# A four-block transformer and GRU kernel: the last block's conditioning moved into the top-k stage, its first rows kept on chip, value projections in four banks, recurrent weights split by GpSimd

## The reference

```python
x = x + _L0_cond_ref(fside_BxSx1_0, cond_2048[:, None, :], x, 5120)     # mask of the 5120 largest of 512x512
x = _L1_cond_ref(x, ...)    # rmsnorm(x)*(1+scale)+shift, qkv, 16 heads of 32, softmax, o + o @ W_out, added to x
x = x + _L2_cond_ref(cond_2048, x, ...)   # a GRU over 512 steps, state 512, weights W_ih and W_hh 512x1536
x = _L3_cond_ref(x, cond_2048, ...)
# L3: ada = (timestep_embed @ ada_w + ada_b);  shift1, scale1, gate1, shift2, scale2, gate2 = split(ada, 6)
#     x1 = ln(x)*(1+scale1)+shift1;  qkv = x1 @ qkv_w + qkv_b;  16 heads of 128;  attn_out @ out_w + out_b
#     x = x + gate1*attn_out;  x2 = ln(x)*(1+scale2)+shift2
#     h = gelu(x2 @ ffn_w1 + ffn_b1);  x = x + gate2*(h @ ffn_w2 + ffn_b2)
```

## Time and profile before

| | |
|---|---|
| median of three runs | 4207.34 us |
| profiled execution | 4210.57 us (span 4208.9 us) |
| top-k stage | 0 to 311.9 us |
| small attention | 311.9 to 971.4 |
| splitting of GRU weights | 971.4 to 998.0 |
| gate inputs | 998.0 to 1152.7 |
| GRU, 512 steps and turning back | 1152.7 to 2594.9 |
| conditioning of the last block | 2594.9 to 2639.5 |
| last block | 2639.5 to 4208.9 |
| PE busy | 3731.0 us (89%) |
| DVE busy | 2778.2 us (66%) |
| ACT busy | 2086.6 us (50%) |
| POOL busy | 461.4 us (11%) |

### The profile page before, as it was taken

One profiled execution on the slowest core, in us unless ns is written; L12 is line 12 of the kernel. 1 busy time (PEld: TensorE's weight loads), 2 busy tenths in 40 slices (PEclk: granted clock), 3 DMA queues, 4 the chain that ended last, 5 costly groups with the idle time before them and its releaser, 6 DMA issues. The chain is left out here.

```text
span 4208.9 us, 177781 instructions
## 1 busy us (share of the span) xinstructions
PE 3731.0 (89%) x70140; PEld 2793.1 (66%) x70140; DVE 2778.2 (66%) x10585; ACT 2086.6 (50%) x7601; POOL 461.4 (11%) x397
## 2 busy tenths in 40 slices
PE   0537888876899999999999998799999999999999
PEld 0424564553499999999999996366456545654664
DVE  6886787785677777777777775376347626743762
ACT  2007786785755555555555552254235324532542
POOL 4005374370000000000000000000100100010001
PEclk9999999998955555555555556899999999999999
DMA  2002131231000000000000004310231122122102
GB/s 90 0 23 69 57 122 59 64 116 61 1 6 6 6 6 6 6 6 6 6 6 6 6 6 172 142 45 16 88 133 45 41 105 90 30 81 116 44 16 90
DMA packets 114611, 209.69 MB, mean 50 GB/s; under 512 B 44154, under 2 KB 76922, under 8 KB 112000
## 3 DMA queue, kind: packets, MB, share of 16 engines
q1 hardware_dynamic: 114436, 207.35, 14.5%
HBM read 165.35 MB, written 33.57 MB: 47 GB/s over the span
## 5 line engine op out<-in xcount | busy, mean ns | idle before, releaser
L1366 PE MATMUL gru_sum_n<-gru_state_parts,w_hh_hi 128*128 128x8 f16 x8192 | 500.2, 175 | 0.0
L1356 PE MATMUL gru_sum_n<-gru_state_parts,w_hh_lo 128*128 128x4 f16 x8192 | 489.4, 168 | 0.0
L1366 PEld LDWEIGHTS gru_sum_n<-gru_state_parts,w_hh_hi 128*128 128x128 f16 x8192 | 376.7, 104 | 0.0
L1356 PEld LDWEIGHTS gru_sum_n<-gru_state_parts,w_hh_lo 128*128 128x128 f16 x8192 | 376.7, 104 | 0.0
L528 ACT ACTIVATE dit_prob<-dit_bank,dit_head_nbias 128x512 f32<-128x512 f32 x256 | 176.0, 688 | 352.2 <-DVE dit_head_nbias L546 351.8
L1499 DVE TENSOR_TENSOR_SCAN gru_n_in<-gru_reset_gate,gru_sum_n 128x32 f32<-128x32 f32 x1024 | 225.5, 220 | 54.6
L1356 PE MATMUL gru_sum_rb<-gru_state_parts,w_hh_lo 128*128 128x4 f16 x4096 | 261.3, 169 | 0.0
L1366 PE MATMUL gru_sum_za<-gru_state_parts,w_hh_hi 128*128 128x8 f16 x4096 | 254.5, 169 | 0.0
L1366 PE MATMUL gru_sum_zb<-gru_state_parts,w_hh_hi 128*128 128x8 f16 x4096 | 254.5, 169 | 0.0
L1366 PE MATMUL gru_sum_ra<-gru_state_parts,w_hh_hi 128*128 128x8 f16 x4096 | 254.5, 169 | 0.0
L1356 PE MATMUL gru_sum_zb<-gru_state_parts,w_hh_lo 128*128 128x4 f16 x4096 | 252.4, 166 | 0.0
(11 more groups left out here) (320 smaller groups left out, 12547.4 us busy)
## 6 DMA issues: line engine op xcount, KB each, us to landing
dit_w_qk<-w_qk_parts SPq DMA_DIRECT2D x64, 512.0 KB, 3.7
weights<-w_parts SPq DMA_DIRECT2D x8, 4096.0 KB, 12.6
weights<-w_out_parts SPq DMA_DIRECT2D x5, 4096.0 KB, 15.6
weights<-w_v_parts SPq DMA_DIRECT2D x5, 4096.0 KB, 12.2
small_given_w<-in_L_cond_qkv_w SPq DMA_DIRECT2D x48, 256.0 KB, 3.1
w_qk_parts<-small_parts_w SPq DMA_DIRECT2D x32, 256.0 KB, 2.1
small_given_w<-in_L_cond_ffn_w SPq DMA_DIRECT2D x32, 256.0 KB, 3.7
w_parts<-small_parts_w SPq DMA_DIRECT2D x32, 256.0 KB, 2.4
```

The costliest lines, as they stand in the source:

```text
L1356: mm = pe.matmul(columns[:, j, 0], w_hh[1][:, k, c:c + P], parts[:, par, 0, k, :, LAST], start=opens, stop=False, skip_group_check=True)
L1366: mm = pe.matmul(columns[:, j], w_hh[0][:, k, c:c + P], parts[:, par, :, k, :, LAST], start=opens, stop=False, skip_group_check=True)
```

## The change

- The last block's conditioning moves into the top-k stage, behind the small attention's conditioning. SP loads ada_w in six pieces of 1 MB into the space of the search's keys, once the search is over; ACT takes the rows from PSUM and adds biases as it writes the columns; DVE adds the gates' bias at the end of the ranking and SP stores the gates. The stage `dit_condition_phase` is gone.
- One piece of SBUF, `room`, 128 KB per partition, is used in turn by the top-k's values and keys, small attention's intermediate tiles, the gate inputs of the GRU and the last block's weights. `given` (batch 0's rows) is allocated outside the stages.
- Small attention's value projections go to `bank[0]` to `bank[3]`, without waits between them; ACT first finishes all queries and keys and then copies the four value banks; DVE takes the low parts last.
- W_hh is split by GpSimd inside the gate-input stage, in eight pieces of 128x768, two behind each batch's copies of X. `split_weights` handles W_ih alone.
- At the end of the GRU SP loads out_w and the value weights into `room` as soon as the last gate inputs are taken. Batches are turned back in the order 1, 2, 3, 0, and batch 0 stays in `given`.
- In the last block PE maps the value bias (48 products, now 128 rows wide, in bank 7) in two halves around the turning of the first rows. DVE adds the result to the bias rows before values are projected. GpSimd's first work of a batch waits for `yl_ready`. out_w is loaded at the end of the batch before.

```diff
@@ topk_phase, sync
+            ada_w = a["L3_cond_ada_w"].rearrange("(k p) n -> p k n", p=P)
+            for i, j in enumerate(CHUNKS):
+                if i >= 4:
+                    sp.wait_ge(ada_rows, i - 3)
+                sp.dma_start(ada[i % 4], ada_w[:, :, j * D:(j + 1) * D]).then_inc(ada_loaded[i % 4], 16)
...
+            sp.wait_ge(gate_added, 1)
+            sp.dma_start(gates_dram, row[:, 4:6, :]).then_inc(gates_stored, 16)
+            sp.wait_ge(gates_stored, 16)
@@ topk_phase, scalar
+            for i in range(6):
+                act.wait_ge(ada_rows, i + 1)
+                act.activation(row[:, i, :], row_sum[i % 2][0:B, :], ACT.Copy).then_inc(row_ready, 1)
+            act.wait_ge(ada_cols, 1)
+            for i in range(4):
+                for f in range(KD):
+                    act.activation(dit_mod[:, i, f, :], col_sum[:, i, f, :], ACT.Identity, scale=XS,
+                                   bias=ada_shift[:, i, f:f + 1]).then_inc(dit_mod_made, 1)
@@ topk_phase, tensor
+            for i in range(6):
+                pe.wait_ge(ada_loaded[i % 4], 16 * (i // 4 + 1))
+                if i >= 2:
+                    pe.wait_ge(row_ready, i - 1)
+                for k in range(KD):
+                    mm = pe.matmul(row_sum[i % 2][0:B, :], c_T[:, k, :], ada[i % 4][:, k, :], start=(k == 0),
+                                   stop=(k == KD - 1))
+                mm.then_inc(ada_rows, 1)
...
@@ topk_phase, vector
+            for i in range(4):
+                dve.tensor_scalar(ada_shift[:, i], ada_b[:, CHUNKS[i] * KD:(CHUNKS[i] + 1) * KD],
+                                  1.0 if i in (SCALE1, SCALE2) else 0.0, XS, ALU.add, ALU.mult)
...
+            dve.wait_ge(row_ready, 6)
+            dve.wait_ge(gate_b_loaded, 32)
+            dve.tensor_tensor(row[:, 4:6, :], row[:, 4:6, :], gate_b, ALU.add).then_inc(gate_added, 1)
@@ small_attention_phase
+        out_of = [qkv_bank[n % 2] if n < first_v else bank[t] for n, (t, j) in enumerate(projections)]
...
-                    pe.wait_ge(bank_free, b * 12 + n + 1)
-                    if n >= first_v + 2:
-                        pe.wait_ge(vl_ready, b * TT + (n - first_v))
+                    if n < first_v:
+                        pe.wait_ge(bank_free, b * first_v + n + 1)
...
-                pe.wait_ge(vl_ready, (b + 1) * TT + 1)
                 pe.wait_ge(lo4_again, (b + 1) * TT * 2)
                 turn_qk(0)
+                pe.wait_ge(vl_ready, (b + 1) * TT)
...
-                    if n == first_v:
+                    if n == first_v - 1:
+                        low_again(TT - 2)
                         root(TT - 1)
-                        low_again(TT - 2)
-                    if n == first_v + 1:
                         high_parts(TT - 1)
-                low_again(TT - 1)
+                        low_again(TT - 1)
@@ gate_input_phase, gpsimd
+            def split_piece(j):
+                k, cols = pieces[j]
+                w = stage[:, j % SLOTS, :]
+                pool.wait_ge(piece_loaded[j % SLOTS], 16 * (j // SLOTS + 1))
+                pool.tensor_scalar(w, w, RS, None, ALU.mult).then_inc(piece_scaled, 1)
+                pool.wait_ge(piece_scaled, j + 1)
+                pool.tensor_copy(w_hh[0][:, k, cols], w).then_inc(piece_hi, 1)
+                pool.wait_ge(piece_hi, j + 1)
+                pool.tensor_tensor(w_hh[1][:, k, cols], w, w_hh[0][:, k, cols], ALU.subtract).then_inc(piece_lo, 1)
...
+                for j in range(b * per_batch, (b + 1) * per_batch):
+                    split_piece(j)
@@ gru_phase, sync
+            for v in range(2):
+                sp.wait_ge(now_loaded[v], 16 * (T // (2 * NOW)))
+            sp.dma_start(region[1], store.out.rearrange("p e k n -> p e (k n)")).then_inc(first_loaded, 16)
+            sp.dma_start(region[0], store.v.rearrange("p e k n -> p e (k n)")).then_inc(first_loaded, 16)
             xo = x_out.rearrange("b (t p) d -> p (b t) d", p=P)
-            for b in range(B):
-                sp.wait_ge(added, (b + 1) * TT)
+            for i, b in enumerate(later[:-1]):
+                sp.wait_ge(added, (i + 1) * TT)
                 sp.dma_start(xo[:, b * TT:(b + 1) * TT, :], X[:, b * TT:(b + 1) * TT, :]).then_inc(stored, 16)
-            sp.wait_ge(stored, 16 * B)
+            sp.wait_ge(stored, 16 * (B - 1))
@@ dit_phase
-            sp.dma_start(given[:], x_rows[:, 0, :, :]).then_inc(x_loaded, 16)
...
+            def map_bias(heads):
+                for h in heads:
+                    left = lambda v: v[:, h:h + 1].broadcast_to([P, P])
+                    mm = products(pe, bank[7][:], (left(bvh), left(bvl)), (w_out[:, 0, h, :], w_out[:, 1, h, :]),
+                                  h == 0, h == H - 1)
+                return mm
+
+            pe.wait_ge(bv_ready, 1)
+            pe.wait_ge(wo_loaded, 16)
+            map_bias(range(H // 2))
             turn_rows(0)
+            map_bias(range(H // 2, H)).then_inc(mapped, 1)
+            pe.wait_ge(rows_ready, 1)
...
+                pool.wait_ge(yl_ready, (b + 1) * KD)
                 pool.wait_ge(gates_loaded, (b + 1) * 16)
```

272 lines of the change are left out of this document (125 added, 147 removed).

## The result

Four runs of the changed kernel took 4129.34 to 4134.21 us, median 4132.31, beside 4209.41 of the kernel before (4205.28 to 4212.84); the ratio is 0.9814, 95% interval 0.9802 to 0.9826. Forecast were 4138, range 4123 to 4162. A second set of four runs gave 4130.57 to 4137.85, median 4132.71, ratio 0.9817 (0.9801 to 0.9834).

A forecast was written before the change was run, and what follows sets the result against it. TensorE is busy 89% of the span, but barriers separate stages, so edits were priced per stage: +2.8 - 16.2 - 10.9 + 4 - 49.2 = -69.5, from 4210.6 to 4141.1 us; 3.2 lower for the median, forecast 4138, range 4123 to 4162.

The forecast's parts named there:

- Top-k: Top-k stage: added conditioning hides beside VectorE's ranking; gates' bias add and store behind it cost +2.8 us.
- Small attention: Small attention: four value projections without waits start each batch's heads 4.05 us earlier, -16.2 us in four batches.
- The third rival: Small attention's units: TensorE stays at the lower clock, up to +108 us, 4246; chance 0.02.
- Splitting: Splitting of the GRU's weights: the stage ends after W_ih alone, -10.9 us, bounds -12 and -8.
- Gate inputs: GRU's gate inputs: GpSimd's splitting of W_hh slows VectorE beside it, +4 us, bounds 0 and +27.
- L1166 loses 0.8 - 0.5 = 0.3 in some four cycles a batch: Gate inputs: fixed 0.8 us per VectorE instruction beside GpSimd, half a microsecond spare; 16 x 0.3 = 5 us.
- the first rival: Gate inputs: GpSimd shuts VectorE out, the stage grows 14 to 27 us, not 4; about 4152, chance 0.12.
- GRU's end: GRU's end: region loads, then three stores ending about 2590.4; last block's first SP issue at 2595.5 us.
- The second rival: GRU's end: queues move 237 GB/s, not 425, so the last block starts 22 us later; 4160, chance 0.12.
- Start of the last block: Last block's start: the first value product begins 22.4 us after the stage's first SP issue.
- the bias decides: Last block's start: mapping the value bias, not the rows' shorter chain, sets the first value product, by 2 us.
- The rest of the last block: Last block's stage: its share of the -49.2 us forecast for GRU's end and the block's start, -5.2 us.

The follow-up runs named there:

- the kernel with two banks: The changed kernel with small attention's value projections in two banks again, copies and low parts in the order of before: 4150.98 us.
- twenty tiny ones: The changed kernel with twenty 4x4 products on TensorE behind the conditioning in top-k, results unread: 4122.36 us.
- the same again: The changed kernel run and profiled a second time with no edit: median 4132.71 us.
- four subtractions: The changed kernel with each of GpSimd's eight subtractions for W_hh done four times: 4135.27 us.
- values late: The changed kernel with the value weights (4.2 MB) loaded in the last block's stage behind its parameters, not at the GRU's end: 4131.22 us.
- one product: The changed kernel with one product instead of the 48 that map the value bias, its share of the output left out: 4132.56 us.
- the large products: The changed kernel with twenty more large float32 products on TensorE in top-k, behind the last block's conditioning, results unread: 4123.07 us.

## Why the prediction held, term by term

- *Top-k*, +2.8 (its terms as written add up to 2.7): +3.5 and +3.2. The order of events was as told; the store's way to the next stage was 0.8 us longer than the earlier trace rows gave for another store.
- *Small attention*, -16.2: the four banks bring 4.5 and not 4.05 in a batch, 18 in all, as the kernel with two banks shows; the stall, which no row of before has, takes 1.3 to 5 back. The third rival (the clock stays low in the units) did not come: the heads of a batch take 103.3 to 103.9 us in both kernels.
- *Splitting*, -10.9: -10.6 and -9.9.
- *Gate inputs*, +4: nothing that can be told, and 153.5 and 154.9 us where the prediction looked for 155 to 160. The step that failed is "L1166 loses 0.8 - 0.5 = 0.3 in some four cycles a batch" as a cost of the stage. L2115's growth stood for a price per instruction; measured it is 0.14 in the mean, and VectorE's idle time takes it. The same idle time is why the first rival fell.
- *GRU's end*: the stage starts 13.7 us behind the first store, where 14.8 were forecast. The second rival fell: beside the GRU's last steps the region loads moved at 401 GB/s, not 237, as the stretch from their issue to the first store says:

```profile
2538.00:2555.00 17.00, 15.74 (x441) 14.81 (x438) 11.96 (x72) 7.61 (x48) 0.00 (x0) 0.50 0.97 401
```

- *Start of the last block*: 22.3 against 22.4. The agreement to 0.1 is luck, since unedited starts spread from 21.95 to 23.94. That the bias decides, by about 2 us, holds: without it the values come 1.3 to 3.3 us sooner.
- *The rest of the last block*: its -5.2 came to -6.4 and -9.5. Beyond the forecast are the dips of the clock, four in before, three and one in the changed kernel, at 1.5 us each; the wait for w_qk, for which nothing was forecast, went from 4.3 and 3.9 to 4.7 and 4.8.
- *Not in the sum*: 4.5 us in the loop of the GRU. With it the sum would have been -74.

So the mechanisms held, and the error of 7.6 us has these parts: +4 charged for a contention that an idle engine absorbed, 4.5 from a loop whose instructions the change leaves as they were, and 1 to 4 in the last block, mostly the clock; against them the stall took back up to 5 that nobody had forecast. That the whole came within 6 us of 4138 owes something to that.

## What to carry to other kernels

A price per instruction, taken from where two engines meet, is a cost of the stage only if the slower one has no idle time there: read its idle column before adding it up. When an edit's gain does not match its mechanism, run the same number of instructions without the work; here twenty tiny ones gave the whole 10 us. And what is small and needed first is better issued ahead of what is large: the parameters behind 8.4 MB cost 10.5 us here, the head weights behind the next batch's rows 4.7 us of waiting at most.

## What was not expected of the hardware

- The same TensorE instructions stall for 2.6 to 3.0 us at one place in some executions and not in others, in this batch or that. Behind three of the six stalls seen (in the changed kernel, in the same again and with four subtractions) the clock stands at 0.50 for a while, behind the other three (values late, and both of one product) it does not.
- The jump back of the GRU's loop of four steps takes either 2.79 or 2.84 us; 124 of 127 are long in the kernel before, 25 to 42 in every variant of the changed kernel, with the same instructions in the loop.
- Work ahead of a pause does not carry the clock over it: with the large products TensorE is busy at 1.00 until 314.5 us, stands at 0.50 between 319 and 325, and is at 0.57 with its first projections from 336 on.
- Behind the same wait of 2.6 us in the last block the clock falls in one execution of a kernel and not in the next, for 1.5 us each time.
